# RWKV attention and a gated expert layer: one gate for the last batch instead of two, a rewritten end, and a different place for the key weights' low parts

## The chip, the cores and the metric

One core of a Trainium2 chip runs the whole kernel. The metric is the device time of one execution in microseconds (us). The kernel before takes 455.28 us, the median of three runs (455.16 to 455.67).

## The reference, cut to what matters

The input x has 8 batches of 512 tokens with 512 features, all float32. One layer of attention and one of experts follow each other, each with a residual sum and a normalisation over the features:

```
key = x*mk + shifted*(1-mk);  value = x*mv + shifted*(1-mv);  rec = x*mr + shifted*(1-mr)
k = key @ Wk;  v = value @ Wv;  r = sigmoid(rec @ Wr)
out = wkv(k, v)            # a scan over the tokens: running maximum, numerator, denominator
x = layernorm(x + (r * out) @ Wo)
logits = x @ router.T ;  gate = softmax(logits), kept for the top 2 of 8 experts
h = x @ down.T             # 8 experts x 16 = 128 columns
x = layernorm(x + (silu(h) * gate) @ up)
```

`shifted` is x moved by one token. Ties between experts go to the lower index.

## The kernel before, in words

**Tiles.** A batch has four chunks of 128 features for the attention and four tiles of 128 tokens for the rest. Tiles are counted through: batch 7, the last, has tiles 28 to 31, batch 6 has 24 to 27, batch 5 has 20 to 23. In the code `t5`, `t6`, `t7` are tiles 20, 24 and 28. There are 32 slots, one for each chunk of each batch: slot s does keys, values and receptances of one chunk (`key`, `value`, `rec` on TensorE), the scans over the tokens (VectorE) and the exponentials (ScalarE). Beside it run the output projection and the experts of earlier batches.

**Matmuls.** Batch 0 multiplies in float32 (`whole`), where one product is two passes (the profile counts x2). From batch 1 on, `split` writes each factor as a high part in the type fp32r and a low part, and makes three single passes of it: high by high, low weights by high, high weights by low. For this WKH and WKL must hold the high and low parts of Wk; ScalarE makes WKH, and two VectorE instructions in the slots 0 and 1 make WKL (L1095, `low_weights(lo)` in the VectorE program, 1,024 columns each). The same for Wv and Wr is done by GpSimd (L1283). The mixes (L970) give key, value and rec of the next batch; in slots 0 and 1 VectorE does two key mixes of batch 1 each.

**Order.** Nothing here is scheduled by a planner: each engine runs its own list, written out by hand, and waits on semaphores. An engine never takes a later instruction first, so a wait holds all that is queued behind it.

**The end.** After slot 31 come, written out tile by tile, the projections of tiles 28 to 31 (`project_high`, `project_low`, `project_rest`), their residual sums (`residual`, L991), means and scales (`moments`, `spread`, ScalarE and VectorE), `normalise` (GpSimd, L1264), transposes (`turn`, L443), their copy (`turned`, ScalarE), the product with router and down weights (`hidden`, L461), its copy (`hidden_copy`), and then the gate:

- `ffn_in` (ScalarE): silu's exponentials and the softmax's exponential,
- `gate_scores` (L1022, L1024) and `gate_top` (L1042 to L1060) on VectorE: maximum, ranks of the experts, the weights of the best two,
- `silu` (L1071, L1075): h times sigmoid, times gate; it releases `agd`,
- `ffn_turn` (TensorE, L480) transposes the result, `ffn_out` (ScalarE) copies it to DQ, and `ffn_up` (L513 for batches 6 and 7, L508 to L510 for batch 5) is the product with the up weights, one per tile,
- `residual2` (L996), the second scale (`spread2`, `square2`, `root2`, `moments2`), `normalise2` (GpSimd, L1269) and the store.

The last batch has two gates, one for tiles 28 and 29 and one for 30 and 31: `STEPS` has an entry for each, and `Part(k)` holds their places. Part 6 is batch 6, parts 7 and 8 are the two halves of batch 7.

```python
STEPS = [(b, 0, NT) for b in range(LAST)] + [(LAST, 0, NT // 2), (LAST, NT // 2, NT)]
```

The expert products of batches 5 and 6 also lie in this end, as work for TensorE between the steps of batch 7.

Of the kernel before, what the change touches and what calls it, by code (L numbers as in the profile page):

```python
# [29 lines left out]
def rwkv_moe_postln(nc, x, xt, vec, wk, wv, wr, wo, dr, up, tri, out):  # L30
    with ExitStack() as ctx:
# [83 lines left out]
        STEPS = [(b, 0, NT) for b in range(LAST)] + [(LAST, 0, NT // 2), (LAST, NT // 2, NT)]  # L115
        spare = EX[:, :, :].rearrange("p a t -> p (a t)")

        def step_of(t):
            b, n = divmod(t, NT)
            return b + (b == LAST and n >= NT // 2)  # L120

        class Part:
            def __init__(self, k):
                self.b, lo, hi = STEPS[k]
# [13 lines left out]
                self.turned_at = ((PK[0], PH)[lo // 2] if tail else PP if k == LAST - 1 else PU)[:, 0:128 * (hi - lo)]  # L138
# [4 lines left out]
        PARTS = [Part(k) for k in range(len(STEPS))]  # L143
# [23 lines left out]
        def up_at(t):  # L167
            if t // NT == LAST:
                return tail_bank(t, PT, PK[0], PK[1], PV)
            if t // NT == LAST - 1:  # L170
                return tail_bank(t, PV, PR, PP, PU)
            return tail_bank(t, PU, PT, PK[0], PU) if t // NT == LAST - 2 else PU[:, :]
# [67 lines left out]
        def _(eng):  # L240
# [40 lines left out]
            eng.wait_ge(q["lwk"], 2)  # L281
# [39 lines left out]
        def _(eng):  # L321
# [9 lines left out]
            def split(dst, weights, high, low, u, which, freed):  # L331
# [4 lines left out]
                if b == 1:  # L336
                    eng.wait_ge(q["hw"], which + 1)
                    eng.wait_ge(q[("lwk", "lwv", "lwr")[which]], j + 1 if which else 2)
# [108 lines left out]
            def hidden(t):  # L447
# [5 lines left out]
                elif b == LAST and n == 1:  # L453
                    eng.wait_ge(q["agc"], LAST)
# [10 lines left out]
            def ffn_turn(k):  # L465
                p = PARTS[k]
                eng.wait_ge(q["agd"], k + 1)
                if k > LAST:
                    eng.wait_ge(q["res"], NT * NB)
                elif k == LAST:  # L470
                    eng.wait_ge(q["res2"], NT * (LAST - 2) + 3)
                elif k == LAST - 1:
                    eng.wait_ge(q["res"], NT * LAST + 1)
# [9 lines left out]
            def ffn_up(t):  # L483
# [9 lines left out]
                if b == LAST and n == 0:  # L493
                    eng.wait_ge(q["res2"], NT * (LAST - 2) + 2)
                elif b == LAST and n == NT - 1:
# [5 lines left out]
                elif b == LAST - 2 and 0 < n < NT - 1:  # L501
                    eng.wait_ge(q["res"], NT * LAST + 1 + n)
# [97 lines left out]
        def _(eng):  # L600
# [300 lines left out]
        def _(eng):  # L901
# [166 lines left out]
            def silu(k):  # L1068
                p = PARTS[k]
                eng.wait_ge(q["sg"], k + 1)  # L1070
                eng.tensor_tensor(p.tiled(p.s1), p.tiled(p.s1), p.hs[:, :, 0:EI], ALU.mult).then_inc(q["sh"], 1)  # L1071
                eng.wait_ge(q["sh"], k + 1)
# [19 lines left out]

            def low_weights(lo):
                eng.wait_ge(q["hw"], 1)
                eng.tensor_tensor(WKL[:, lo:lo + 2, :], X1T[:, lo:lo + 2, :], WKH[:, lo:lo + 2, :].bitcast(F32),  # L1095
                                  ALU.subtract).then_inc(q["lwk"], 1)
# [8 lines left out]
            for s in SLOTS:  # L1105
# [38 lines left out]
                if s < 2:  # L1144
                    mixes(1, 0, 2 * s, 2 * s + 1)
# [6 lines left out]
                if s < 2:  # L1152
                    low_weights(2 * s)
# [239 lines left out]
```

## Time and profile before

| | |
|---|---|
| median of three runs | 455.28 us |
| the profiled execution | 455.12 us |
| its span, first to last instruction | 453.3 us |
| TensorE (PE) busy | 442.3 us, 98% |
| VectorE (DVE) busy | 404.6 us, 89% |
| ScalarE (ACT) busy | 363.7 us, 80% |
| GpSimd (POOL) busy | 313.0 us, 69% |
| TensorE's granted clock, mean | 0.995 |

The profile gives for each instruction its start from the span's start and its duration. Instructions of one engine overlap a little: the next one starts before the end of the one before, so the distance of two starts is what a queue pays for one. "L991" is line 991 of the kernel before. A tile's name stands for all buffers of that name (PK for PK0 and PK1). A row "PE PK<-KH,WKH" is a matmul into PK; a float32 matmul counts as two.

### The profile page before, as it was taken

The numbers are of one execution on the slowest core, as the hardware profiler recorded it, in microseconds if no ns is written. First come the engines' busy times: TensorE is split into PE (matmuls) and PEld (weight loads), VectorE is DVE, ScalarE is ACT, GpSimd is POOL, SyncE is SP. The second block draws the span as 40 slices with busy tenths as digits, with TensorE's granted clock in tenths as the row PEclk, the third lists the DMA queues.
The fourth block names the chain that finished last, engine by engine and source line by source line (L and its number), as shares of the span: only waits on it lengthen the run. The fifth ranks groups of instructions, "written<-read, shape, count | busy, mean of one in ns | idle before, by whom it ended". The sixth has DMA issues, their size and how long they took to land. (4 is left out here: it accounts for less than half of the span.)

```text
span 453.3 us, 6683 instructions
## 1 busy us (share of the span) xinstructions
PE 442.3 (98%) x1984; PEld 340.7 (75%) x1984; DVE 404.6 (89%) x614; ACT 363.7 (80%) x810; POOL 313.0 (69%) x298
## 2 busy tenths in 40 slices
PE   8999999999999999999999999999999999999993
PEld 3444667778888888888888888888888888878771
DVE  6999999898888989999899989999899996875985
ACT  7877668877888779888788789888789887668695
POOL 0455786688657997579867898579966794753335
PEclk9999999999999999999999999999999999999998
DMA  8603320042000042003320042100520023400016
GB/s 250 217 1 119 116 69 1 1 140 72 0 1 0 25 163 88 6 0 99 113 71 0 1 158 78 45 0 25 163 94 0 4 68 94 140 1 0 1 48 231
DMA packets 20244, 30.64 MB, mean 68 GB/s; under 512 B 2032, under 2 KB 7152, under 8 KB 20208
## 3 DMA queue, kind: packets, MB, share of 16 engines
q1 hardware_dynamic: 20064, 29.95, 20.5%
q8 instruction: 16, 0.26, 0.2%
q10 hardware_dynamic: 144, 0.26, 0.2%
q14 instruction: 20, 0.16, 0.1%
HBM read 21.82 MB, written 8.39 MB: 67 GB/s over the span
## 5 line engine op out<-in xcount | busy, mean ns | idle before, releaser
L604 ACT ACTIVATE PR<-PR 128x512 f32<-128x512 f32 x128 | 74.5, 582 | 29.0 <-DVE PR L948 9.6
L1255 POOL TENSOR_TENSOR DQ<-DEN,EX 128x512 f32<-128x512 f32 x32 | 41.9, 1310 | 23.6 <-DVE DEN L919 23.6
L1261 POOL TENSOR_SCALAR NM<-SUM,RS 128x1 f32<-128x1 f32 x30 | 7.9, 264 | 59.8 <-ACT RS L604 59.8
L342 PE MATMUL PK<-KH,WKH 128*128 128x512 f32 x112 | 46.5, 415 | 0.4 <-DVE NUM L936 0.4
L970 DVE SCALAR_TENSOR_TENSOR KT<-D,VEC,XT 128x512 f32<-128x512 f32 x56 | 46.3, 874 | 0.0
L342 PE MATMUL PV<-VH,WVH 128*128 128x512 f32 x112 | 45.4, 406 | 0.0
L342 PE MATMUL PR<-RH,WRH 128*128 128x512 f32 x112 | 44.3, 395 | 0.2 <-DVE RW L960 0.2
L348 PE MATMUL PK<-KL,WKH 128*128 128x512 f32 x112 | 44.1, 394 | 0.0
L348 PE MATMUL PV<-VL,WVH 128*128 128x512 f32 x112 | 44.1, 394 | 0.0
L348 PE MATMUL PR<-RL,WRH 128*128 128x512 f32 x112 | 44.0, 393 | 0.0
L343 PE MATMUL PK<-KH,WKL 128*128 128x512 f32 x112 | 43.8, 391 | 0.0
L343 PE MATMUL PR<-RH,WRL 128*128 128x512 f32 x112 | 43.7, 390 | 0.0
L343 PE MATMUL PV<-VH,WVL 128*128 128x512 f32 x112 | 43.7, 390 | 0.0
L1223 POOL TENSOR_TENSOR VL<-KT,VH 128x512 fp32r<-128x512 f32 x28 | 38.9, 1410 | 4.0 <-ACT VH L604 4.0
L1223 POOL TENSOR_TENSOR RL<-D,RH 128x512 fp32r<-128x512 f32 x27 | 39.5, 1492 | 3.0 <-ACT RH L604 2.9
L919 DVE TENSOR_TENSOR_SCAN DEN<-PK,EX 128x512 f32<-128x512 f32 x32 | 38.9, 1217 | 2.6 <-issue 1.4
L604 ACT ACTIVATE EX<-EX 128x512 f32<-128x512 f32 (+1 forms) x66 | 40.3, 610 | 0.0
L936 DVE TENSOR_TENSOR_SCAN NUM<-PK,EX 128x512 f32<-128x512 f32 x32 | 39.2, 1224 | 1.1
L906 DVE TENSOR_TENSOR_SCAN M<-CST,PK 128x512 f32<-128x512 f32 x32 | 38.7, 1211 | 0.0
L604 ACT ACTIVATE PK<-PK 128x512 f32<-128x512 f32 x64 | 38.3, 598 | 0.0
L371 PE MATMUL PP<-WOH,TH 128*128 128x512 f32 x88 | 35.9, 407 | 0.0
L1223 POOL TENSOR_TENSOR KL<-KT,KH 128x512 fp32r<-128x512 f32 x28 | 35.2, 1293 | 0.0
(289 smaller groups left out, 1276.0 us busy)
## 6 DMA issues: line engine op xcount, KB each, us to landing
XT<-in_xt SPq DMA_DIRECT2D x32, 256.0 KB, 3.7
XN<-in_x SPq DMA_DIRECT2D x28, 256.0 KB, 2.7
out<-XN SPq DMA_DIRECT2D x28, 256.0 KB, 2.0
X1T<-in_wo SPq DMA_DIRECT2D x1, 1024.0 KB, 5.5
XT<-in_x SPq DMA_DIRECT2D x4, 256.0 KB, 3.6
out<-XT SPq DMA_DIRECT2D x3, 256.0 KB, 2.3
X1T<-in_wk SPq DMA_DIRECT2D x2, 256.0 KB, 5.0
XN<-in_wv SPq DMA_DIRECT2D x2, 256.0 KB, 5.5
```

Source lines behind the costliest of these rows:

```text
L342: eng.matmul(dst[:, :], wh[:, c, o], high[:, c, :], start=(c == 0), stop=False)
L343: eng.matmul(dst[:, :], wl[:, c, o], high[:, c, :], start=False, stop=False)
L348: last = eng.matmul(dst[:, :], wh[:, c, o], low[:, c, :], start=False, stop=(c == C - 1))
L371: eng.matmul(projected_at(t), high(c), WOH[:, c, :], start=(c == 0), stop=False)
L604: eng.activation(*a, **k).then_inc(q[s], 1)
L906: eng.tensor_tensor_scan(M[:, 1:T + 1], TD[:, j:j + 1].to_broadcast([128, T]), PK[u % 2][:, :], NEG, ALU.add, ALU.max).then_inc(q["m"], 1)
L919: eng.tensor_tensor_scan(DEN[:, 1:T + 1], PK[u % 2][:, :], EX[:, 0, :], 0.0, ALU.mult, ALU.add)\
L936: eng.tensor_tensor_scan(NUM[:, 1:T + 1], PK[u % 2][:, :], EX[:, 0, :], 0.0, ALU.mult, ALU.add)\
L970: eng.scalar_tensor_tensor(out=full(b, which, c), in0=D[:, c, :], scalar=VEC[:, 2 + which, c:c + 1], in1=XT[:, c, 0:T], op0=ALU.mult, op1= ...
L1223: eng.tensor_tensor(lo[:, c, :], full(b, which, c), hi[:, c, :].bitcast(F32), ALU.subtract)\
L1255: eng.tensor_tensor(DQ[:, :], DEN[:, 0:T], EX[:, 1, :], ALU.add).then_inc(q["e"], 1)
L1261: eng.tensor_scalar(NM1[:, col(t)], total, RS1[:, col(t)], scale, ALU.mult, ALU.mult)\
```

## The change

Four things are done, and no arithmetic is left out.

1. **Gate.** `STEPS` goes; batch 7 has one part for its four tiles. `ffn_in`, `gate_scores`, `gate_top`, `silu`, `ffn_turn` and `ffn_out` of batch 7 run once, on operands of twice the columns.
2. **Key weights.** The two VectorE instructions for WKL go. GpSimd makes WKL in slot 0, in four instructions of the form it has for WVL, after the first `denominator` and the differences of batch 1. It first waits until the fourth key mix of batch 1 is done.
3. **Key mixes.** All four key mixes of batch 1 stand in slot 0, none in slot 1. TensorE's keys and the load of Wo wait for four counts of `lwk` instead of two.
4. **End.** The lists of TensorE, ScalarE, VectorE and GpSimd after slot 31 stand in another order, `silu` is cut into `silu_of` and `silu_gated`, and three products use other banks (tile 21 of `ffn_up` PH instead of PT, the transposes of batch 6 PT instead of PP).

The diff, cut to its core:

```diff
-        STEPS = [(b, 0, NT) for b in range(LAST)] + [(LAST, 0, NT // 2), (LAST, NT // 2, NT)]
         def step_of(t):
-            b, n = divmod(t, NT)
-            return b + (b == LAST and n >= NT // 2)
+            return t // NT
...
-                self.turned_at = ((PK[0], PH)[lo // 2] if tail else PP if k == LAST - 1 else PU)[:, 0:128 * (hi - lo)]
+                self.turned_at = (PK[0] if tail else PT if k == LAST - 1 else PU)[:, 0:128 * (hi - lo)]
...
@@ TensorE, end @@
-            ffn_up(t5)
             project_high(t7 + 3)
             project_low(t7 + 3)
             project_rest(t7 + 3)
+            ffn_up(t5)
             turn(t7)
-            ffn_turn(LAST - 1)
+            ffn_up(t5 + 1)
             turn(t7 + 1)
             hidden(t7)
-            ffn_up(t5 + 1)
             turn(t7 + 2)
             hidden(t7 + 1)
+            turn(t7 + 3)
             ffn_up(t5 + 2)
-            turn(t7 + 3)
             hidden(t7 + 2)
+            ffn_turn(LAST - 1)
+            hidden(t7 + 3)
             ffn_up(t5 + 3)
-            hidden(t7 + 3)
-            ffn_up(t6)
+            for t in range(t6, t7):
+                ffn_up(t)
             ffn_turn(LAST)
-            ffn_up(t6 + 1)
-            ffn_up(t6 + 2)
-            ffn_turn(LAST + 1)
-            ffn_up(t6 + 3)
             for t in range(t7, NT * NB):
                 ffn_up(t)
...
@@ ScalarE, end @@
+            spread(t7 + 2)
             turned(t7)
-            spread(t7 + 2)
-            ffn_out(LAST - 1)
-            spread2(t5)
+            spread(t7 + 3)
             turned(t7 + 1)
             hidden_copy(t7)
-            spread(t7 + 3)
             turned(t7 + 2)
             hidden_copy(t7 + 1)
+            turned(t7 + 3)
+            square2(t5, JUNK[:, :])
+            hidden_copy(t7 + 2)
+            ffn_out(LAST - 1)
+            root2(t5, 1)
+            hidden_copy(t7 + 3)
             ffn_in(LAST)
-            turned(t7 + 3)
-            hidden_copy(t7 + 2)
             spread2(t5 + 1)
             square2(t5 + 2, JUNK[:, :])
-            hidden_copy(t7 + 3)
-            ffn_in(LAST + 1)
-            ffn_out(LAST)
             square2(t5 + 3, KT[:, 0, :])
             root2(t5 + 2, 2)
-            ffn_out(LAST + 1)
             spread2(t6, 2)
+            ffn_out(LAST)
             spread2(t6 + 2, 2)
...
@@ VectorE, slots 0 and 1 @@
-                if s < 2:
-                    mixes(1, 0, 2 * s, 2 * s + 1)
+                if s == 0:
+                    mixes(1, 0, 0, 1, 2, 3)
...
-                if s < 2:
-                    low_weights(2 * s)
...
@@ VectorE, end @@
             residual(t7)
-            silu(LAST - 1)
             residual(t7 + 1)
             moments(t7 + 1)
             residual(t7 + 2)
-            residual2(t5)
+            silu_of(LAST - 1)
             residual(t7 + 3)
             moments(t7 + 3)
+            silu_gated(LAST - 1)
+            residual2(t5)
             residual2(t5 + 1)
             moments2(t5 + 1)
+            residual2(t5 + 2)
             gate_scores(LAST)
-            residual2(t5 + 2)
+            residual2(t5 + 3)
             gate_top(LAST)
-            silu(LAST)
-            residual2(t5 + 3)
-            gate_scores(LAST + 1)
-            gate_top(LAST + 1)
-            silu(LAST + 1)
-            for n in range(NT):
-                residual2(t6 + n)
+            residual2(t6)
+            residual2(t6 + 1)
+            silu_of(LAST)
+            silu_gated(LAST)
+            residual2(t6 + 2)
+            residual2(t6 + 3)
...
@@ GpSimd, slot 0 and end @@
+                if s == 0:
+                    eng.wait_ge(q["kt"], 3 * C + C)
+                    low_weights(0, *range(C))
...
-            for n in range(NT - 1):
+            for n in range(NT):
                 normalise(t7 + n)
-            normalise2(t5)
-            normalise(t7 + 3)
-            for t in range(t5 + 1, NT * NB):
+            for t in range(t5, NT * NB):
```

**Where instructions move, VectorE in slots 0 and 1.** Before:

```order
L948 SCALAR_TENSOR_TENSOR PR<-PR,DQ 128x512
L970 SCALAR_TENSOR_TENSOR KT<-D,VEC,XT 128x512 x2
L1095 TENSOR_TENSOR WKL<-X1T,WKH 128x1024
L960 TENSOR_TENSOR RW<-NU,PR 128x512
L919 SCALAR_TENSOR_TENSOR DEN<-PK,EX 128x512
```

Now (the lines have other numbers, the instructions are the same):

```order
L938 SCALAR_TENSOR_TENSOR PR<-PR,DQ 128x512
L960 SCALAR_TENSOR_TENSOR KT<-D,VEC,XT 128x512 x4
L950 TENSOR_TENSOR RW<-NU,PR 128x512
L909 SCALAR_TENSOR_TENSOR DEN<-PK,EX 128x512
```

In slot 0 one WKL instruction is replaced by two mixes; slot 1, which read like the first block too, now has neither.

**VectorE at the end**, from the residual sum of tile 22 (XN1<-PK0) to the last gate's product DEN. EX holds scores and weights of batch 7, NUM the comparisons, M and DEN the two products of silu. Before, the second gate and what is ahead of it:

```order
L1071 TENSOR_TENSOR M<-M,EX 128x256
L1075 TENSOR_TENSOR DEN<-M,EX 128x256
L996 TENSOR_TENSOR XN1<-PU,XN1 128x512
L1022 TENSOR_REDUCE EX<-EX 128x2
L1024 TENSOR_TENSOR EX<-EX 128x16
L1042 TENSOR_TENSOR NUM<-EX 128x128
...
L1060 SCALAR_TENSOR_TENSOR EX<-EX 128x16
L1071 TENSOR_TENSOR M<-M,EX 128x256
L1075 TENSOR_TENSOR DEN<-M,EX 128x256
L996 TENSOR_TENSOR XN0<-PV,XN0 128x512
```

Now:

```order
L986 TENSOR_TENSOR XN1<-PK0,XN1 128x512
L1012 TENSOR_REDUCE EX<-EX 128x4
L1014 TENSOR_TENSOR EX<-EX 128x32
L986 TENSOR_TENSOR XN1<-PU,XN1 128x512
L1032 TENSOR_TENSOR NUM<-EX 128x256
...
L1050 SCALAR_TENSOR_TENSOR EX<-EX 128x32
L986 TENSOR_TENSOR XN0<-PV,XN0 128x512
L986 TENSOR_TENSOR XN0<-PR,XN0 128x512
L1061 TENSOR_TENSOR M<-M,EX 128x512
L1068 TENSOR_TENSOR DEN<-M,EX 128x512
```

Three residual sums (tile 23, then tiles 24 and 25) now stand between the last scores and the product that releases the last transposes.

**TensorE at the end**, its last instructions. Before:

```order
L461 MATMUL PP<-DR,D 128x136 x4
L513 MATMUL PV<-KT,NU 128x512
L480 MATMUL PK<-IDN,DEN 128x128 x2
L513 MATMUL PR<-KT,NU 128x512
L513 MATMUL PP<-KT,NU 128x512
L480 MATMUL PH<-IDN,DEN 128x128 x2
L513 MATMUL PU<-KT,NU 128x512
L513 MATMUL PT<-KT,DQ 128x512
L513 MATMUL PK<-KT,DQ 128x512 x2
L513 MATMUL PV<-KT,DQ 128x512
```

Now:

```order
L459 MATMUL PP<-DR,D 128x136 x4
L502 MATMUL PU<-UPH,AGH 128x512
L503 MATMUL PU<-UPL,AGH 128x512
L504 MATMUL PU<-UPH,AGL 128x512
L507 MATMUL PV<-KT,NU 128x512
L507 MATMUL PR<-KT,NU 128x512
L507 MATMUL PP<-KT,NU 128x512
L507 MATMUL PU<-KT,NU 128x512
L476 MATMUL PK<-IDN,DEN 128x128 x4
L507 MATMUL PT<-KT,DQ 128x512
L507 MATMUL PK<-KT,DQ 128x512 x2
L507 MATMUL PV<-KT,DQ 128x512
```

The product of tile 27 (PU<-KT,NU) stood between the last transposes and the four products of batch 7; now nothing does.

## Rows read from the trace of the kernel before

**Rows 1.** Waits of TensorE over the whole span (us in total, times, longest)

```profile
PE PV L443 <- POOL XT L1264: 0.9, 1, 0.9
PE PK L342 <- DVE NUM L936: 0.4, 1, 0.4
```

**Rows 2.** VectorE in time, start of the program (start us, us, engine, line, operation)

```profile
22.76 1.40 DVE L970 SCALAR_TENSOR_TENSOR KT<-D,VEC,XT 128x512 f32<-128x512 f32 x2
24.08 1.22 DVE L1095 TENSOR_TENSOR WKL<-X1T,WKH 128x1024 fp32r<-128x1024 f32 x1
...
29.80 0.69 DVE L943 TENSOR_TENSOR NU<-NUM,PV 128x512 f32<-128x512 f32 x1
...
36.32 1.23 DVE L919 TENSOR_TENSOR_SCAN DEN<-PK,EX 128x512 f32<-128x512 f32 x1
```

**Rows 3.** TensorE in time, start of the program

```profile
30.95 3.60 PE L328 MATMUL PV<-RW,XN 128*128 128x512 f32 x8
```

**Rows 4.** GpSimd in time, start of the program

```profile
28.38 5.02 POOL L1283 TENSOR_TENSOR WVL<-XN,WVH 128x512 fp32r<-128x512 f32 x4
```

**Rows 5.** ScalarE in time, start of the program

```profile
35.65 0.59 ACT L604 ACTIVATE PK<-PK 128x512 f32<-128x512 f32 x1
```

**Rows 6.** TensorE in time, end of the program

```profile
428.65 0.60 PE L443 MATMUL PK<-IDN,XT 128*128 128x128 f32 x4
...
430.56 0.63 PE L443 MATMUL PV<-IDN,XT 128*128 128x128 f32 x4 [0.88 <-POOL XT L1264]
...
438.23 1.02 PE L513 MATMUL PV<-KT,NU 128*128 128x512 f32 x2
...
442.69 1.02 PE L513 MATMUL PT<-KT,DQ 128*128 128x512 f32 x2
443.54 1.88 PE L513 MATMUL PK<-KT,DQ 128*128 128x512 f32 x4
445.26 1.02 PE L513 MATMUL PV<-KT,DQ 128*128 128x512 f32 x2
```

**Rows 7.** VectorE in time, end of the program

```profile
421.78 0.41 DVE L1042 TENSOR_TENSOR KT<-HS 128x256 f32<-128x256 f32 x1
422.11 1.54 DVE L1043 TENSOR_TENSOR KT<-HS 128x256 f32<-128x256 f32 x1
...
425.14 0.68 DVE L991 SCALAR_TENSOR_TENSOR XT<-PP,XT 128x512 f32<-128x512 f32 x1
...
425.75 0.68 DVE L1071 TENSOR_TENSOR KT<-KT,HS 128x512 f32<-128x512 f32 x1
426.47 0.69 DVE L1075 TENSOR_TENSOR KT<-KT,GS 128x512 f32<-128x512 f32 x1
...
435.75 0.28 DVE L1042 TENSOR_TENSOR NUM<-EX 128x128 f32<-128x128 f32 x1
...
437.29 0.42 DVE L1071 TENSOR_TENSOR M<-M,EX 128x256 f32<-128x256 f32 x1
...
441.07 0.42 DVE L1075 TENSOR_TENSOR DEN<-M,EX 128x256 f32<-128x256 f32 x1
...
445.46 0.69 DVE L996 TENSOR_TENSOR XT<-PK,XT 128x512 f32<-128x512 f32 x1 [0.17 <-PE PK L513]
```

**Rows 8.** ScalarE in time, end of the program

```profile
430.96 0.58 ACT L604 ACTIVATE NU<-PP 128x512 f32<-128x512 f32 x1
...
438.43 0.28 ACT L604 ACTIVATE EX<-PP 128x136 f32<-128x136 f32 x1 [0.23 <-PE PP L461]
```

**Rows 9.** The chain that ended last, its last row

```profile
449.12 0.72 ACT XT L604
```

**Rows 10.** GpSimd in time, end of the program

```profile
437.68 1.04 POOL L1269 TENSOR_SCALAR XN<-XN,RS,ZERO 128x512 f32<-128x512 f32 x1 [2.85 <-ACT RS L678]
```

**Rows 11.** After the last matmul: stretch, busy PE, PEld, DVE, ACT, POOL, granted clock, DMA

```profile
448.00:449.00 1.00, 0.00 (x0) 0.00 (x0) 0.96 (x3) 0.49 (x3) 1.00 (x2) 1.00 0.95 352
449.00:450.00 1.00, 0.00 (x0) 0.00 (x0) 0.00 (x0) 0.81 (x2) 0.63 (x1) 0.54 0.64 240
```

More of the change, by code:

```diff
@@ L112, in col @@
             return slice(i, i + 1)
-        STEPS = [(b, 0, NT) for b in range(LAST)] + [(LAST, 0, NT // 2), (LAST, NT // 2, NT)]
         spare = EX[:, :, :].rearrange("p a t -> p (a t)")
         def step_of(t):
-            b, n = divmod(t, NT)
-            return b + (b == LAST and n >= NT // 2)
+            return t // NT
         class Part:
             def __init__(self, k):
-                self.b, lo, hi = STEPS[k]
+                self.b, lo, hi = k, 0, NT
                 self.tiles, self.n = range(NT * self.b + lo, NT * self.b + hi), hi - lo
@@ L137, in __init__ @@
                 self.agt = (DQ if tail else NU if k == LAST - 1 else AGH)[:, 128 * lo:128 * hi]
-                self.turned_at = ((PK[0], PH)[lo // 2] if tail else PP if k == LAST - 1 else PU)[:, 0:128 * (hi - lo)]
+                self.turned_at = (PK[0] if tail else PT if k == LAST - 1 else PU)[:, 0:128 * (hi - lo)]
             def tiled(self, a):
                 return a.rearrange("p (n h) -> p n h", n=self.n)
-        PARTS = [Part(k) for k in range(len(STEPS))]
+        PARTS = [Part(k) for k in range(NB)]
         def tail_bank(t, *banks):
@@ L171, in up_at @@
                 return tail_bank(t, PV, PR, PP, PU)
-            return tail_bank(t, PU, PT, PK[0], PU) if t // NT == LAST - 2 else PU[:, :]
+            return tail_bank(t, PU, PH, PK[0], PU) if t // NT == LAST - 2 else PU[:, :]
         MEASURED = [NT * (LAST - 2) + 1, NT * LAST + 2, NT * LAST + 3]
@@ L280, in _ @@
             eng.dma_start(TRI[:, :], tri).then_inc(q["tri"], 16)
-            eng.wait_ge(q["lwk"], 2)
+            eng.wait_ge(q["lwk"], C)
             eng.wait_ge(q["k"], C)
@@ L337, in split @@
                     eng.wait_ge(q["hw"], which + 1)
-                    eng.wait_ge(q[("lwk", "lwv", "lwr")[which]], j + 1 if which else 2)
+                    eng.wait_ge(q[("lwk", "lwv", "lwr")[which]], j + 1)
                 for c in range(C):
@@ L453, in hidden @@
                 elif b == LAST and n == 1:
-                    eng.wait_ge(q["agc"], LAST)
+                    eng.wait_ge(q["res"], NT * LAST + 1)
                 elif b == LAST:
@@ L467, in ffn_turn @@
                 eng.wait_ge(q["agd"], k + 1)
-                if k > LAST:
-                    eng.wait_ge(q["res"], NT * NB)
-                elif k == LAST:
+                if k == LAST:
                     eng.wait_ge(q["res2"], NT * (LAST - 2) + 3)
                 elif k == LAST - 1:
-                    eng.wait_ge(q["res"], NT * LAST + 1)
+                    eng.wait_ge(q["res"], NT * LAST + 2)
                 elif k == LAST - 2:
@@ L492, in ffn_up @@
                     eng.wait_ge(q["agl"], k + 1)
-                if b == LAST and n == 0:
-                    eng.wait_ge(q["res2"], NT * (LAST - 2) + 2)
-                elif b == LAST and n == NT - 1:
+                if b == LAST and n == NT - 1:
                     eng.wait_ge(q["res2"], NT * (LAST - 1) + 1)
@@ L501, in ffn_up @@
                 elif b == LAST - 2 and 0 < n < NT - 1:
-                    eng.wait_ge(q["res"], NT * LAST + 1 + n)
+                    eng.wait_ge(q["res"], NT * LAST + 5 - n)
                 elif LAST - 2 <= b < LAST and n:
@@ L1066, in gated_low, with silu_of @@
                    .then_inc(q["agl"], 1)
-            def silu(k):
+            def silu_of(k):
                 p = PARTS[k]
@@ L1071, in silu, with silu_gated @@
                 eng.tensor_tensor(p.tiled(p.s1), p.tiled(p.s1), p.hs[:, :, 0:EI], ALU.mult).then_inc(q["sh"], 1)
+            def silu_gated(k):
+                p = PARTS[k]
                 eng.wait_ge(q["sh"], k + 1)
@@ L1091, in _ @@
             eng.tensor_scalar(QB, CC, -1.0, CLIP, ALU.mult, ALU.add).then_inc(q["cc"], 1)
[L1093 to L1096, printed above, removed]
             first_mixes(0, 0, 1)
@@ L1278, in low_weights @@
             def low_weights(i, *blocks):
-                stage, high, low, done = ((XN[0], WVH, WVL, "lwv"), (XN[1], WRH, WRL, "lwr"))[i - 1]
+                stage, high, low, done = ((X1T, WKH, WKL, "lwk"), (XN[0], WVH, WVL, "lwv"), (XN[1], WRH, WRL, "lwr"))[i]
                 eng.wait_ge(q["hw"], i + 1)
```

## The prediction

> **What bounds the kernel now.** I read TensorE's waits first: in the whole span it waits hardly at all, and the two longest waits inside it are 0.9 and 0.4 us [rows 1]. So up to about 428 us the kernel is TensorE's stream, and its matmuls don't change. A change of VectorE's list can only gain there what those waits hold. Then the chain that ended last, which closes with ScalarE's scaling of tile 31 at 449.12 [rows 9]; followed back it runs over VectorE's residual sums and TensorE's last four products, the first at 442.69 [rows 6]. VectorE's sum of tile 30 at 445.46 waited for them [rows 7]. So the end is set by when those products start, and the second gate's DEN, done at 441.07 + 0.42 = 441.49 [rows 7], is what lets them.
>
> **The start.** Removed from VectorE: two WKL instructions of 1.22 us. Moved from slot 1 to slot 0: two mixes, 1.40 us a pair [rows 2]. Slot 0 pays 1.4 - 1.2 = 0.2 us more, slot 1 about 2.6 us less. Neither reaches the end:
> - The 0.2 us: VectorE's NU of slot 1 ends at 29.80 + 0.69 = 30.49 [rows 2], and the values that wait for it start at 30.95 [rows 3]. With 0.2 us more it is still 0.25 us early. If that cover is gone, TensorE waits by the excess, at most 0.2 us in each of a few slots; I take 0, with +0.3 as the upper end.
> - The 2.6 us: VectorE's next scan is DEN at 36.32, and ScalarE's exponential that it needs ends at 35.65 + 0.59 = 36.24 [rows 2, 5]. VectorE becomes free at 34 and waits. I take 0; the lower end is the 0.4 us wait for VectorE later on [rows 1].
> - GpSimd: four WKL instructions of the form of the WVL ones, 5.02 us for four [rows 4]. They start when the fourth mix ends, 22.76 + 4 x 0.7 = 25.5, and end at 30.5; the DQ instruction behind them, then WVL, end near 31.8 and 36.8, 3.4 us later than now (28.38 + 5.02 = 33.4). The keys that need WKL come only after four slots of batch 0, and the next work of GpSimd hangs on DEN at 36.32 + 1.23. The load of Wo waits for `lwk` and for the keys of slot 3, and the latter stays last. The cover here is over 0.5 us at each place. Cost 0.
>
> **The end, TensorE up to the last hidden product.** From tile 28's transposes at 428.65 to the first product of batch 6 at 438.23 TensorE does, in another order, the same instructions as after the change [rows 6]; ahead of 428.65 too, since only `ffn_up(t5)` and the projection of tile 31 change places. Of these 9.58 us, 0.88 is a wait for GpSimd's normalised tile 29 [rows 6]. It falls away: ScalarE no longer copies tile 28's transposes and squares tile 30 ahead of what GpSimd needs, and a 0.8 us product fills the gap (it waits some 0.2 us for the residual sum of tile 31). By the distances of the starts I also count 0.5 us of small waits for copies less, since each copy now lies ahead of two instructions. The block takes 8.2 us, and hidden(31) is now followed by one 0.8 us product. So its copy, which ended at 438.43 + 0.28 = 438.71 [rows 8], ends at **436.6**, 2.1 us earlier; 437.1 if the small waits stay.
>
> **The end, VectorE to the last gate's product.** In front of DEN, from the copy on:
> - scores 0.4 us, to 437.0;
> - residual2 of tile 23, 0.6 us (a sum of this size costs the queue 425.75 - 425.14 = 0.61 [rows 7]), to 437.6;
> - gate_top on four tiles: batch 6's took from 421.78 to 425.14 = 3.36 us, with one comparison at 1.54 where its twin took 0.41 [rows 7]. That one ran beside a GpSimd instruction on two tensors, which the new place does not have: 3.36 - 1.13 = 2.23 us, to 439.85;
> - residual2 of tiles 24 and 25, 1.2 us, to 441.05;
> - the two silu products on 512 columns, 426.47 - 425.75 + 0.69 = 1.41 us [rows 7], to **442.46**.
>
> ScalarE's part (`ffn_in`) needs 2.5 us from 436.6 and is done at 439.2, beside gate_top. So `agd` comes 442.46 - 441.49 = 0.97 us later than the second gate's does now. Two gates cost VectorE more in all than one, but the last of two needs only 441.49 - 438.71 = 2.8 us behind the last copy, and this one 5.9.
>
> **From there to the end.** Four transposes, 0.60 us, then the copy of 512 columns, 0.58 [rows 6, 8], with 0.1 us between: the first product of batch 7 starts at 443.8 in place of 442.69, **+1.1 us**. TensorE's four products of batch 6 run straight behind the block, 436.9 + 4 x 0.86 = 440.3, so it is idle from then on; now the product of tile 27 covers the second gate's copy, and that makes the 0.1 us on top. The four products, 0.85 us each (443.54 - 442.69 [rows 6]), the sums, moments, root, scaling and the store follow unchanged, so 1.1 us reaches the end. GpSimd's last stores come no later than they do now.
>
> **Sum.** 0 + 1.1 us on the profiled 455.12 gives 456.2; the median of the runs is 0.16 above that execution, so for medians **456.4 us**, 0.25% slower. The line between this and no change is 0.2%, 0.9 us, about what a measurement of this kernel can tell. The term's own bounds: the copy at 437.1 adds 0.5; without the wait at 437 for the sum of tile 23 it is 0.6 less. This case alone spans 455.8 to 457.3.
>
> **Rivals.**
> - *The gate is cheaper than its columns.* The two-tile gate_top took 437.29 - 435.75 = 1.54 us [rows 7]. If four tiles cost the same, 0.7 us are saved; with silu nearer its small form (0.78 for two), 1.3. The sum is then -0.2: no change, 455.1. Against it: the same instructions took 0.41 on 256 columns and 0.28 on 128 [rows 7]. Chance 0.18.
> - *The head start carries through, faster.* The place is VectorE between the last copy and DEN. If besides the cheap gate the sums of tiles 24 and 25 cost nothing, since VectorE would have waited there for ScalarE's sigmoid anyway, `agd` comes at 439.9, and the end 1.4 us sooner: 453.9. It decides from `agd` earlier than 441.4. For it: the last copy is 2.1 us earlier. Against it: by the durations ScalarE is done before gate_top. Chance 0.10.
> - *TensorE's clock.* The new gap, 440.3 to 443.8 with only transposes in it, is longer than any before the last product now. In the trace the granted clock is still 1.00 in 448 to 449, more than 1.7 us after the last matmul (445.26 + 1.02 = 446.28 [rows 6]), and 0.54 in 449 to 450 [rows 11]. If it falls in the gap, the four products take 1.7 us each in place of 0.86: +3.4 more, 459.8. Against it: the gap is broken by transposes. Chance 0.12.
> - *The port of VectorE and GpSimd.* GpSimd's `normalise2` of tile 22 becomes ready at 441.4, between the two silu products. In the trace that same meeting, GpSimd at 437.68 between M at 437.29 and DEN, stretched GpSimd to 1.04 us and left VectorE's products alone (M 0.42, as in the other gate's DEN) [rows 7, 10]. So I take 0. But VectorE did lose 1.13 us once to a GpSimd instruction [rows 7], so this might be +0.7, 457.1; chance 0.05.
>
> The Trainium skill (SBUF — State Buffer, section "SBUF: two separate sides") has a VectorE instruction with two SBUF inputs and a GpSimd instruction exclude each other for the whole of one, the first to start going first. By that rule the second product could wait for all of a 0.8 us `normalise2`; the 1.54 us comparison agrees with the rule, and the row at 437.68 shows GpSimd as the one that waits. By the same rule WKL on GpSimd would cost VectorE something only beside mixes, and none is left there.
>
> **How the numbers follow.** The main case has 0.55, of which 0.08 stays within 0.9 us. Slower: 0.47 + 0.12 + 0.05 = 0.64. Within 0.2%: 0.08 + 0.18 = 0.26. Faster: 0.10. The range 454.8 to 457.7 takes in the main case, the cheap gate and the port, and leaves out the clock and most of the faster case, 0.2 in all.
>
> **What would show it.** Right: TensorE without the 0.9 us wait at 430; the last copy near 436.6; VectorE waiting before the scores; gate_top some 2.2 us; DEN ending near 442.5; a TensorE gap of about 2 us before the last four transposes; the first of the last four products at 443.8; unchanged starts of the slots of batch 1. Wrong: DEN before 441.5, matmuls of batch 7 at twice their duration, or TensorE waiting for NU or WKL before 60 us.

## The result, and the profile after

The changed kernel takes **459.33 us** (median of 6 runs, 458.33 to 460.17) beside 455.29 us for the kernel before on the same chip (6 runs, 454.99 to 455.67): ratio 1.0085, 95% interval 1.0067 to 1.0102. So it is slower, by nearly four times what was predicted (4.0 us, not 1.1), and outside the range. The profiled execution took 460.08 us, its span is 458.3; the kernel before has 455.12 and 453.3.

The 5.0 us between the two spans, read from the start of tile 28's transposes on, since up to there TensorE does the same matmuls:

| stretch | before | after | difference | predicted |
|---|---|---|---|---|
| span's start to tile 28's transposes | 428.65 | 429.02 | +0.37 | 0 |
| from there to the first product of batch 7 | 14.04 | 16.33 | +2.29 | +1.1 |
| from there to ScalarE's last scaling | 6.43 | 9.18 | +2.75 | 0 |
| from there to the span's end | 4.18 | 3.77 | -0.41 | 0 |

The -0.41 fits the stores: from the last scaling on fewer are left. Before, the shares of the DMA engines in the four microseconds from 449 on add up to 3.0 (0.64, 1.02, 1.03, 0.35), now in the four from 454 on to 2.1 (0.00, 0.74, 1.02, 0.33).

TensorE's waits in the changed kernel (us in total, times, longest), against [rows 1]:

```profile
PE PK L476 <- DVE DEN L1068: 2.7, 1, 2.7
...
PE PT L507 <- ACT DQ L595: 0.7, 1, 0.7
PE PK L340 <- DVE NUM L926: 0.4, 1, 0.4
PE PH L502 <- DVE XT L981: 0.4, 1, 0.4
```

The wait of 0.9 us for GpSimd's normalised tile 29 is gone, as predicted. A wait of 2.7 us for the gate's product and one of 0.7 for its copy have taken its place. TensorE in time, to be read against [rows 6] (a bracket at the end of a row is the engine's idle time just ahead of it, and what ended it):

```profile
429.02 0.60 PE L441 MATMUL PK<-IDN,XT 128*128 128x128 f32 x4
430.04 0.47 PE L502 MATMUL PH<-UPH,AGH 128*128 128x512 f32 x1 [0.42 <-DVE XT L981]
...
437.67 1.02 PE L507 MATMUL PV<-KT,NU 128*128 128x512 f32 x2
...
440.25 1.02 PE L507 MATMUL PU<-KT,NU 128*128 128x512 f32 x2
443.94 0.72 PE L476 MATMUL PK<-IDN,DEN 128*128 128x128 f32 x4 [2.68 <-DVE DEN L1068]
445.35 2.07 PE L507 MATMUL PT<-KT,DQ 128*128 128x512 f32 x2 [0.69 <-ACT DQ L595]
447.21 3.62 PE L507 MATMUL PK<-KT,DQ 128*128 128x512 f32 x4
450.62 1.33 PE L507 MATMUL PV<-KT,DQ 128*128 128x512 f32 x2
```

TensorE stands still from 440.25 + 1.02 = 441.27 to 443.94. The first product of batch 7 starts at 445.35 in place of 442.69, and then two products of two matmuls take 2.07 and 1.33 us and four matmuls 3.62, where [rows 6] have 1.02, 1.02 and 1.88. VectorE, against [rows 7]:

```profile
428.27 1.02 DVE L1061 TENSOR_TENSOR KT<-KT,HS 128x512 f32<-128x512 f32 x1
429.21 0.68 DVE L981 SCALAR_TENSOR_TENSOR XT<-PH,XT 128x512 f32<-128x512 f32 x1
```
```profile
437.49 0.19 DVE L1012 TENSOR_REDUCE EX<-EX 128x4 f32<-128x32 f32 x1 [1.92 <-ACT EX L595]
...
438.60 0.41 DVE L1032 TENSOR_TENSOR NUM<-EX 128x256 f32<-128x256 f32 x1
...
440.83 0.68 DVE L986 TENSOR_TENSOR XN<-PV,XN 128x512 f32<-128x512 f32 x1
...
442.03 0.68 DVE L1061 TENSOR_TENSOR M<-M,EX 128x512 f32<-128x512 f32 x1
442.75 1.14 DVE L1068 TENSOR_TENSOR DEN<-M,EX 128x512 f32<-128x512 f32 x1
...
447.46 0.69 DVE L986 TENSOR_TENSOR XT<-PT,XT 128x512 f32<-128x512 f32 x1 [2.37 <-PE PT L507]
```

After it waited for the last hidden copy (ScalarE's, below), VectorE doesn't pause until DEN ends, at 442.75 + 1.14 = 443.89. Later it waits 2.37 us for the slow products. ScalarE's last copy and its last scaling, against [rows 8, 9], and GpSimd's scaling of tile 21 (its first row) and of tiles 22 and 23 (the second):

```profile
437.17 0.28 ACT L595 ACTIVATE EX<-PP 128x136 f32<-128x136 f32 x1
...
454.53 0.72 ACT L595 ACTIVATE XT<-XT,RS 128x512 f32<-128x512 f32 x1
```
```profile
440.61 0.79 POOL L1256 TENSOR_SCALAR XN<-XN,RS,ZERO 128x512 f32<-128x512 f32 x1 [2.58 <-ACT RS L669]
442.42 2.11 POOL L1256 TENSOR_SCALAR XN<-XN,RS,ZERO 128x512 f32<-128x512 f32 x2 [1.03 <-ACT RS L680]
```

The stretches of the end (busy PE, PEld, DVE, ACT, POOL, then TensorE's granted clock, DMA share, GB/s), against [rows 11]:

```profile
443.00:444.00 1.00, 0.06 (x1) 0.06 (x2) 1.00 (x2) 0.82 (x4) 1.00 (x2) 1.00 0.04 12
444.00:445.00 1.00, 0.66 (x4) 0.36 (x4) 1.00 (x2) 0.44 (x2) 1.00 (x2) 0.70 0.70 262
445.00:450.00 5.00, 4.65 (x6) 2.07 (x7) 1.47 (x3) 2.75 (x10) 2.55 (x4) 0.50 0.65 240
450.00:451.00 1.00, 1.00 (x2) 0.45 (x2) 0.13 (x1) 0.82 (x3) 0.00 (x0) 0.50 0.30 111
451.00:452.00 1.00, 0.95 (x2) 0.00 (x0) 0.97 (x2) 0.20 (x1) 0.70 (x1) 0.88 0.00 0
```

The granted clock is 1.00 (2.4 GHz) until 444, falls within the next microsecond to 0.50 (1.2 GHz), and stays there until past 451: six of the eight last matmuls run wholly at half the clock. That is the rival that had 0.12.

### The profile page after: what moved, and what is told of

The parts are those of the page before. It is cut to its first block, busy times and chain, and to the rows that moved or that the text cites. A ratio compares the mean times of both kernels' runs of the same rounds, so it can differ in the third digit from the quotient of the medians.

```text
span 458.3 us, 6662 instructions
## 1 busy us (share of the span) xinstructions
PE 445.9 (97%) x1984; PEld 342.5 (75%) x1984; DVE 401.5 (88%) x599; ACT 363.8 (79%) x804; POOL 318.8 (70%) x302
## 4 chain that ended last, share of the span: by engine, by line
PE 79%; DVE 4%; ACT 1%; issue 1%; POOL 1%; ACTq 0%
PE PH L459 6%; PE PV L346 5%; PE PV L340 5%; PE PV L341 5%; PE PK L340 5%; PE PK L346 5%; PE PR L346 5%; PE PK L341 5%; PE PR L341 5%; PE PR L340 5%; PE PP L369 4%; PE PP L374 4%; PE PP L370 4%; PE PT L441 3%; PE PP L389 2%
```

## The experiments

Two questions were open. Is the clock the cause of the 2.75 us, and nothing else? And what is the remaining 2.29 us made of, of which 1.1 was predicted? All the times below are medians; the kernel before took 455.2 to 455.4 in each group. "Behind tile 28" is the distance from the start of tile 28's transposes, which takes out what the start of the program adds or saves.

**The changed kernel again**, beside the next three on one chip.

> The changed kernel once more, to see whether its runs fall into two groups. Theory (the granted clock falls in the gap ahead of the last four products): runs of two kinds, near 458.4 and near 460.1 us, the slower kind with a mean clock of 0.989 and with the four products at some 1.8 us each. Rival (the time comes from the order of work and the shared port alone): one group, and a run with a high mean clock is as long as the others. If a profile of the faster kind is caught, the first of the four products starts where it does in the slow one, near 445.3, and the products are faster.

460.09 us (460.09 to 460.12), ratio 1.0104 (1.0091 to 1.0117), mean granted clock 0.988 in every run. All four runs were of the longer kind. The 458.3 to 458.6 of three of the first runs didn't come up; those had a mean clock of 0.992 to 0.995.

**Unread products in the gap.**

```diff
             for t in range(t6, t7):
                 ffn_up(t)
+            for _ in range(3):
+                eng.matmul(PH[:, :], IDN[:, :], UPT, start=True, stop=True)
             ffn_turn(LAST)
```

> Three float32 products whose result nobody reads (into bank PH, 0.86 us each) run on TensorE between its last product of batch 6 and the four last transposes, where it waited 2.7 us. Clock theory: the clock stays at 1.00, the four products take 0.86 us each, so 3.4 us come back from a run of the slow kind and the time is 456.5 to 457 us in one group. Rival (order and port cost the whole): nothing comes back, 459.3. A third view (filling delays the transposes): first product later than 445.3.

457.14 us (456.88 to 457.21), ratio 1.0038 (1.0026 to 1.0049). TensorE:

```profile
440.94 2.74 PE L586 MATMUL PH<-KT,IDN 128*128 128x512 f32 x6
443.77 0.66 PE L476 MATMUL PK<-IDN,DEN 128*128 128x128 f32 x4
445.12 1.13 PE L507 MATMUL PT<-KT,DQ 128*128 128x512 f32 x2 [0.69 <-ACT DQ L597]
```

The granted clock stays at 1.00 there, the transposes take 0.66 and the first product 1.13. It starts 16.27 us behind tile 28, as in the changed kernel (16.33): work that nobody reads, put where TensorE was idle, moves no other step, and takes 2.95 us off. From the first product to ScalarE's last scaling it is 451.66 - 445.12 = 6.54 us, against 6.43 before and 9.18 in the changed kernel: the clock explains the slower products. What is left, 1.9 us against the kernel before, comes with the later release of the last transposes; the next runs take that apart.

**The start change alone**, on the kernel before (all key mixes of slot 0 together, the key lows on GpSimd; the end as before).

> The kernel before with the change of the start alone (all four key mixes in slot 0, WKL on GpSimd behind them). My theory: no change, 455.3 us, -0.1 to +0.3. Rival (the start is what costs part of the 4 us, as TensorE's values start 0.6 us later in the profile of the changed kernel): 455.9 or more. If the 0.6 us in that profile is only the first eight matmuls (6.27 in place of 5.20 us, whose work did not change), the start varies from run to run in the kernel before as well.

454.98 us (454.72 to 455.79), ratio 0.9993 (0.9984 to 1.0002): no change that this measurement can tell. The order of the end is that of [rows 6], and so are the distances: 443.36 - 429.32 = 14.04.

```profile
429.32 0.60 PE L443 MATMUL PK<-IDN,XT 128*128 128x128 f32 x4
...
443.36 1.02 PE L513 MATMUL PT<-KT,DQ 128*128 128x512 f32 x2
```

**The silu products ahead of two residual sums** (the changed kernel, no filler).

```diff
+            silu_of(LAST)
+            silu_gated(LAST)
             residual2(t6)
             residual2(t6 + 1)
-            silu_of(LAST)
-            silu_gated(LAST)
```

(ScalarE's `ffn_out(LAST)` goes ahead of `spread2(t6, 2)` likewise.)

> The changed kernel with the two silu products of batch 7 ahead of the residual sums of tiles 24 and 25 on VectorE, and the copy of the last transposes ahead of the squares of those tiles on ScalarE. Order theory: the last product of the gate ends 1.2 us earlier and misses the GpSimd instructions that stretched it to 1.14 us, so 1.2 + 0.45 us are gained by the order alone. Clock theory: the wait ahead of the last transposes shrinks from 2.7 to about 1.0 us and the clock does not fall, so another 3.4 us: 455.5 to 456.2 us in all. If the clock falls in spite of it: 457.5 to 458.5.

457.27 us (456.11 to 457.69), ratio 1.0037 (1.0025 to 1.005). The profiled run is the shortest, 456.11:

```profile
442.10 0.66 PE L476 MATMUL PK<-IDN,DEN 128*128 128x128 f32 x4 [1.45 <-DVE DEN L1068]
443.44 1.12 PE L507 MATMUL PT<-KT,DQ 128*128 128x512 f32 x2 [0.69 <-ACT DQ L595]
```
```profile
440.21 1.10 DVE L1061 TENSOR_TENSOR M<-M,EX 128x512 f32<-128x512 f32 x1
441.35 0.69 DVE L1068 TENSOR_TENSOR DEN<-M,EX 128x512 f32<-128x512 f32 x1
```

The two sums cost about what the prediction had for them (1.2): the first product comes 443.44 - 428.41 = 15.03 us behind tile 28, 1.30 sooner. The gap is 1.45 us in place of 2.68, and in this run the clock stayed at 1.00 through it. It didn't in all: of the six runs two took 456.1 and 456.3, and four 457.0 to 457.7. That the clock fell in those four is read from their times alone: no trace of one was kept, and their mean clock of 0.994 hardly differs from the 0.995 of the profiled run. DEN is back at 0.69, and now the product before it, M, has the 1.10: GpSimd's scaling of tile 21 meets that one.

**GpSimd held back** (on the filled kernel: GpSimd waits for the last gate's product before tile 22).

```diff
                 if t not in FINISHED:
+                    if t == t5 + 2:
+                        eng.wait_ge(q["agd"], NB)
                     normalise2(t)
```

> The changed kernel with the three unread products in TensorE's gap (the clock held, 457.14), and GpSimd made to wait for the last gate's product (agd at NB) before normalise2 of tile 22. Theory: in the changed kernel DEN takes 1.14 us in place of 0.69 because GpSimd's normalise2 runs at the same time; with GpSimd held back DEN is 0.69 again, the last four transposes start 0.45 us sooner, and the time is 456.7, ratio 1.0031. Rival: DEN is long for another reason (ScalarE's reads, TensorE's fillers), stays at 1.14, and the time stays at 457.1.

456.70 us (456.28 to 457.32), ratio 1.0034 (1.0022 to 1.0046).

```profile
441.98 0.69 DVE L1070 TENSOR_TENSOR DEN<-M,EX 128x512 f32<-128x512 f32 x1
```

DEN takes 0.69: the stretch was GpSimd's. The first product comes 444.19 - 428.24 = 15.95 us behind tile 28, 0.32 sooner than in the filled kernel, not 0.45: DEN is done at 442.67, but the three unread products keep TensorE until the transposes start at 442.91.

**`silu_of` of batch 6 behind tile 31's residual sum** (on the filled kernel).

```diff
-            silu_of(LAST - 1)
             residual(t7 + 3)
             moments(t7 + 3)
+            silu_of(LAST - 1)
```

> The same base (changed, three unread products), but silu_of of batch 6 behind the residual sum and moments of tile 31 in VectorE's list. Theory: the last hidden copy is late by up to 0.48 us because VectorE does that product, 1.02 us beside a GpSimd instruction, ahead of tile 31's residual sum, and TensorE's ffn_up waits 0.42 for that sum; moved behind, the wait goes, the copy and all behind it come about 0.4 us sooner: 456.7. Rival: the wait only changes its cause (the later copy, or silu_gated and ffn_out of batch 6, now late for its own products), and the time stays at 457.1.

456.62 us (456.34 to 457.06), ratio 1.0031 (1.002 to 1.0042).

```profile
428.33 0.60 PE L441 MATMUL PK<-IDN,XT 128*128 128x128 f32 x4
428.76 0.47 PE L502 MATMUL PH<-UPH,AGH 128*128 128x512 f32 x1
```

`ffn_up` follows the transposes after 0.43 us, without the wait (in the changed kernel 1.02, with 0.42 of wait); the last copy starts 436.12 - 428.33 = 7.79 us behind tile 28 in place of 8.15, the first product 15.91 in place of 16.27.

**All of these at once**, with `ffn_up` of tile 27 behind the last transposes, where it covers their copy, and two unread products. GpSimd waits for the last gate's product already before tile 21 here, and ScalarE's copy goes ahead of `spread2(t6, 2)` again. TensorE's list:

```diff
-            for t in range(t6, t7):
+            for t in range(t6, t6 + 3):
                 ffn_up(t)
+            eng.wait_ge(q["res2"], NT * (LAST - 2) + 3)
+            for _ in range(2):
+                eng.matmul(PH[:, :], IDN[:, :], UPT, start=True, stop=True)
             ffn_turn(LAST)
+            ffn_up(t6 + 3)
```

> All mends at once on the changed kernel: both silu products of the last gate ahead of the residual sums of tiles 24 and 25; silu_of of batch 6 late; GpSimd waits for the last gate's product before normalise2 of tile 21; two unread products in the gap instead of three; and ffn_up of tile 27 behind the last gate's transposes, where it covers ScalarE's copy of them. The theory's terms, each from a run so far: clock 2.95, the two sums 1.2 to 1.4, late copy 0.45, stretched product 0.45. From 457.14 with the clock held: minus 1.2, 0.4, 0.45 gives 455.1, no change against before (ratio 0.9997). Rival: the terms do not add, since the residual sums moved behind the gate now come late for the products of batch 7 that reuse their banks: then 456 or more.

455.43 us (455.14 to 456.06), ratio 1.0007 (0.9999 to 1.0016): as the kernel before.

```profile
441.43 0.66 PE L476 MATMUL PK<-IDN,DEN 128*128 128x128 f32 x4 [0.17 <-DVE DEN L1072]
...
442.78 1.11 PE L507 MATMUL PT<-KT,DQ 128*128 128x512 f32 x2
```

The terms add at the first product: it is 442.78 - 428.52 = 14.26 us behind tile 28, against 14.04 before and 16.27 with the filler alone, so 2.0 us sooner, and 1.2, 0.36 and 0.45 were expected. Of the 2.0 the time shows 1.7 (457.14 to 455.43).

**Two gates in the new order**: the end as changed, but the last batch's gate split again into pairs, `silu_of` of batch 6 late, and ScalarE's squares of tiles 20 and 21 behind the gates. No unread products. `STEPS`, the banks of the last batch's transposes and TensorE's two `ffn_turn` are as in the kernel before. VectorE's list:

```diff
+            gate_scores(LAST)
+            gate_top(LAST)
             residual2(t5 + 2)
-            gate_scores(LAST)
+            silu_of(LAST)
+            silu_gated(LAST)
+            gate_scores(LAST + 1)
             residual2(t5 + 3)
-            gate_top(LAST)
-            residual2(t6)
-            residual2(t6 + 1)
-            silu_of(LAST)
-            silu_gated(LAST)
+            gate_top(LAST + 1)
+            silu_of(LAST + 1)
+            silu_gated(LAST + 1)
+            residual2(t6)
+            residual2(t6 + 1)
```

> The changed kernel's new order of the end up to the last hidden product, but the one gate split again into two of two tiles, as before, and ScalarE's squares of tiles 20 and 21 behind the last gate. Theory: what the one gate costs is that all four tiles' work waits for the last copy; with two gates the first is done ahead of it, and the first of the last four products starts 12.7 to 14 us behind tile 28's transposes in place of 14.04 before and 16.3 now: 454.0 to 455.2, ratio 0.997 to 1.000. Rival: ScalarE (four exponentials, two copies and the postponed squares) becomes the bound at the end, and the time is 456 or more.

455.54 us (455.29 to 456.02), ratio 1.0006 (0.9997 to 1.0015). TensorE, VectorE and ScalarE:

```profile
440.18 0.44 PE L480 MATMUL PH<-IDN,DEN 128*128 128x128 f32 x2 [0.37 <-DVE DEN L1076]
...
441.32 1.02 PE L511 MATMUL PT<-KT,DQ 128*128 128x512 f32 x2
```
```profile
448.66 0.79 DVE L1005 TENSOR_SCALAR XT<-XT,RS 128x512 f32<-128x512 f32 x1 [1.41 <-ACT RS L676]
```
```profile
448.98 0.72 ACT L602 ACTIVATE XT<-XT,RS 128x512 f32<-128x512 f32 x1
```

The first product is 441.32 - 428.58 = **12.74** us behind tile 28: 1.30 sooner than before, 3.59 sooner than in the changed kernel (16.33), and 1.52 sooner than with one gate and every mend (14.26). So the new order, with two gates, gains 1.30 us at this place; joining the gate loses 1.52 of the 3.59, and the other 2.07 are what the mends of the run before took back. But the gain of 1.3 us stops at ScalarE: VectorE stands 1.41 us waiting for its root, and the last scaling starts 20.40 behind tile 28, against 20.47 before. The time lies between the theory's and the rival's; the mechanism at the end is the rival's.

**The same, with the end balanced anew.**

```diff
-        MEASURED = [NT * (LAST - 2) + 1, NT * LAST + 2, NT * LAST + 3]
+        MEASURED = [NT * (LAST - 2) + 1, NT * LAST + 1, NT * LAST + 2, NT * LAST + 3]
...
-            spread2(t7, 2)
-            spread2(t7 + 2)
-            spread2(t7 + 3)
+            spread2(t7)
+            spread2(t7 + 1, 3)
```

(VectorE takes `moments2(t7 + 1)` behind `residual2(t7 + 1)`.)

> Two gates in the new order, as in the run before, with the end balanced anew: tile 29's second moments move from ScalarE (square and sum) to VectorE, which waited 1.41 us there for ScalarE's root, and ScalarE takes the roots of tiles 29 to 31 in one pair of instructions in place of three. Theory: in that run the last products end 1.5 us sooner than before, and ScalarE, busy without a gap from 440.65 to 448.98, hands none of it on; relieved of a square (0.7 us) and of two pairs (0.5 us each), its last scaling starts 0.5 to 0.7 us sooner: 454.9, ratio 0.9987, and no more than the stores allow. Rival: the stores, four in the last 3 us, are the bound, and the time stays at 455.5.

455.29 us (454.93 to 455.88), ratio 0.9998 (0.9989 to 1.0007). The last scaling starts 448.93 - 428.98 = 19.95 us behind tile 28, 0.45 sooner than in the run before, but the span's end comes 453.8 - 448.93 = 4.87 us behind it, where the kernel before has 4.18. The DMA engines (last two columns, share and GB/s) in the last stretches:

```profile
450.00:451.00 1.00, 0.00 (x0) 0.00 (x0) 0.00 (x0) 0.00 (x0) 0.17 (x1) 0.50 0.94 344
451.00:452.00 1.00, 0.00 (x0) 0.00 (x0) 0.00 (x0) 0.00 (x0) 0.00 (x0) 0.50 1.01 383
452.00:453.00 1.00, 0.00 (x0) 0.00 (x0) 0.00 (x0) 0.00 (x0) 0.00 (x0) 0.50 0.92 346
```

They are nearly full until 453, while in the kernel before, where tile 28 came 0.33 us earlier, their share in 452 to 453 is 0.35. GpSimd ends its last scaling 21.2 us behind tile 28 (before: 21.0), so the store behind that one comes no sooner, however early ScalarE is. The rival, the stores as the bound, fits; that a better spread of the stores would bring the rest was not tried.

**One unread product in place of three.**

> The changed kernel with one unread product in TensorE's gap in place of three, so that about 2 us stay idle ahead of the last transposes and 0.7 behind them. Theory: the clock falls with the length of the idle stretch, not because of the products' place; with 1.45 + 0.69 us idle (the silu products first) some runs lost about 1.4 us and some nothing, so here a part of the 2.95 us stays: 458 to 459, in two kinds of runs. Rival: any real product inside the gap keeps the clock: 457.1 in every run.

457.26 us (457.04 to 458.75), ratio 1.005 (1.0036 to 1.0065). Four runs took 457.0 to 457.3, two 458.5 and 458.8; the profiled one is of the latter:

```profile
443.60 0.66 PE L476 MATMUL PK<-IDN,DEN 128*128 128x128 f32 x4 [1.81 <-DVE DEN L1070]
444.94 1.97 PE L507 MATMUL PT<-KT,DQ 128*128 128x512 f32 x2 [0.69 <-ACT DQ L597]
```
```profile
444.00:445.00 1.00, 0.31 (x4) 0.07 (x2) 0.74 (x2) 0.71 (x2) 1.00 (x3) 1.00 0.58 217
445.00:446.00 1.00, 1.00 (x2) 0.48 (x3) 0.00 (x0) 1.00 (x4) 0.70 (x1) 0.54 0.90 330
```

With 1.81 + 0.69 us idle the clock fell to 0.54 in 445 to 446, a microsecond later than in the changed kernel, and came back earlier. A real product in the gap doesn't hold the clock by being there: what stays idle behind it still counts. The rival, 457.1 in every run, fell. Of the theory the two kinds of runs held, but not the 458 to 459: four of six runs lost nothing that shows. The changed kernel without any filler kept three of its five runs on the same chip (below), so these six don't show that one unread product makes a fall rarer.

**The changed kernel on this chip too.**

> The changed kernel itself on this chip, beside the other two. The runs so far gave 460.1 or 458.4 us and nothing between. Theory: the two kinds differ in TensorE's clock alone, and a profile of the shorter kind shows the last products partly at the full rate. 460.1 in most runs; a 458.4 run may or may not come up.

457.02 us (456.83 to 460.19), ratio 1.006 (1.0035 to 1.0084). Neither the theory's 460.1 nor its 458.4: three runs took 456.8 to 457.0 at a mean clock of 0.997 or 0.998, two 459.6 and 460.2 at 0.991 and 0.988. The first three have the time and the mean clock of the filled kernel; none of them was profiled. So by the times the same program with the same gap lost 3 us in two runs and nothing in three; the profile shown is of a run that lost:

```profile
443.52 1.12 PE L476 MATMUL PK<-IDN,DEN 128*128 128x128 f32 x4 [2.69 <-DVE DEN L1068]
```
```profile
443.00:444.00 1.00, 0.48 (x2) 0.48 (x3) 1.00 (x3) 0.53 (x4) 1.00 (x1) 0.50 0.22 84
```

Here the clock was already down when the last transposes ran: 1.12 us, against 0.66 in the filled kernel. The granted clock is 0.50 in all of 443 to 444, and the last product of batch 6 had ended at 439.81 + 1.02 = 440.83: it fell within 2.2 us of it, sooner than in the profile of [rows 11], where it fell some 2.7 us behind the last matmul.

## Why the prediction was wrong

It had the direction and the place. The number failed, since the largest term, the clock, was put down as a rival and left out of the range; of the terms up to the first product four were short as well.

- **The start, at 0: right.** Alone it gives a ratio of 0.9993 (0.9984 to 1.0002). Neither the GpSimd work nor the longer slot 0 shows. The 0.37 us by which tile 28 comes later in the profiled run is within what profiles of the changed start differ by: the twelve of them have tile 28's transposes between 428.24 and 429.32, with the 428.65 of the kernel before inside. TensorE's first eight matmuls, whose work didn't change, took 5.20 us before, 6.27 after, and 4.74 and 6.21 in two other runs of the changed start.
- **The wait of 0.9 us, gone: right.** The 0.2 us expected in its place are 0.42 (`PE PH L502`). The step that failed is the cover: the prediction didn't count that `silu_of` of batch 6 stands ahead of tile 31's residual sum on VectorE and takes 1.02 us beside GpSimd. That and small waits that stayed make the last hidden copy end 8.43 us behind tile 28, not 7.95: **+0.48**, of which moving that product took back 0.36.
- **From the copy to DEN: 1.15 and 2.23 us where 1.0 and 2.23 were predicted.** The four-tile `gate_top` is exact: it runs from 438.60 to 440.83. The 1.54 us comparison that the prediction took out of batch 6's figure did run beside GpSimd:

```profile
422.07 1.30 POOL L1248 TENSOR_TENSOR KL<-RW,KH 128x512 fp32r<-128x512 f32 x1 [2.24 <-ACT KH L604]
```

  With the 2.23 the cheap-gate rival falls. The two residual sums took 1.20, and moving them away gained 1.30. So the second rival, the head start, in which they hide, falls too.
- **The silu products at 1.41: wrong by 0.45.** DEN takes 1.14, and 0.69 with GpSimd held back. "So I take 0" was the failed step: the meeting of [rows 10] was read as harmless because there GpSimd had lost. GpSimd had come second there; here it is ahead of DEN. Its scaling of tile 22, the first of the two in the row at 442.42, began beside the silu product M (442.03) and took 0.93 us, asked for alone, where the one at 440.61 took 0.79; it ended at 443.35. DEN had begun at 442.75 and ended at 443.89, 0.54 us behind GpSimd's end, where it takes 0.69 alone: it had waited for nearly all of the scaling. The Trainium skill (SBUF — State Buffer, section "SBUF: two separate sides") states this for a VectorE instruction with two inputs in SBUF: the one that starts first has the port for its whole instruction. These rows agree with it in who waits, in both orders; by the starts and durations of the rows DEN would have ended at 443.35 + 0.69 = 444.04, 0.15 us later than it did. In the same rows VectorE's sums that read a product from PSUM (440.83, 0.68) aren't stretched beside GpSimd's 440.61.
- **Behind DEN, 1.34 predicted, 1.46 measured.** In all 1.1 + 0.48 + 0.15 + 0.45 + 0.12 = 2.3, and 2.29 is what the table has. With the clock held the kernel takes 456.8 to 457.2 us: inside the range, some 0.6 above the forecast. That it comes so close is in part luck: the first product is 2.2 us late and not 1.1, and the stores give back 0.44 at the end (from the last scaling to the span's end 455.4 - 451.66 = 3.74 us with the filler, 4.18 before), which the prediction had at 0.
- **The clock: 0.12 for what happened, in whole or in part, in 12 of the changed kernel's 15 runs.** The rival was priced at +3.4 and cost 2.95; its 459.8 stands beside 459.33. What failed is how [rows 11] were read. They show 1.00 for 448 to 449 and 0.54 for 449 to 450, that is, a fall some 2.7 us or more behind the last matmul, which had ended at 446.28. The failed step is the overlap: the prediction took only the first half of it ("still 1.00 after 1.7 us") as speaking against, while its own gap, 440.3 to 443.8, was 3.5 us long. And the transposes that were to break the gap stand near its end: even ahead of them it had 440.3 to 442.5. So the rows gave no ground for a chance of 0.12. The Trainium skill (TensorE: Matmul & The Clock Gate, section "Part 1: The HAM clock gate") has the half rate as what an idle TensorE goes to and the two levels as the only ones; the granted clock of 0.50 and matmuls of twice the duration agree.

Why one gate comes later than the last of two: its work is cheap in sum, but all of it waits for the last tile's hidden product. With two, half the gate is done by then, and the first gate's copy and product fill TensorE while the second is worked out. The first product of batch 7 comes 16.33 us behind tile 28 in the changed kernel, 14.26 with one gate and the mended order, and 12.74 with two gates in the new order. Of these 3.59 us the joined gate itself has 1.52 (the two runs behind this also differ in the unread products and in where ScalarE has two squares). The other 2.07 are the order around it: the two residual sums ahead of the silu products (1.2 to 1.3), GpSimd's scaling beside DEN (0.3 to 0.45) and `silu_of` of batch 6 (0.36). Where the clock falls, 2.95 come on top. The kernel before, with its older order, has 1.30 of the 3.59 too. In the whole time the 1.52 us don't show: one gate in the mended order, with two unread products, takes 455.43 us, two gates take 455.54 and the kernel before 455.39; with two gates ScalarE's queue holds the end, and behind it, as far as the runs go, the stores. So what made the changed kernel slow is the gap that it left TensorE and the order around the gate; that joining the gate by itself costs time was not shown.

## What to carry to other kernels

Before work near the end is joined or moved, write down how long TensorE will stand idle just before its last products, and compare that with how long the clock outlived the last matmul in the traces at hand. If the gap comes near it, put the products behind it at twice their duration in one end of the range. A single trace is no safe measure: here it showed 2.7 us, another run had lost the clock within 2.2, and by their times even runs with 1.45 + 0.69 us idle lost some of it. Cheap remedies, in the order in which I would try them: shorten the gap by putting first, on the engine that TensorE waits for, what TensorE needs; move real products into it; and only then unread ones. Of two engines that share a port, ask which will start first, not which lost last time. A gain on TensorE is worth only what the next engine's queue lets through.

## What was not expected of the hardware

- The same program with the same idle gap of 2.7 us kept the clock in three runs (456.8 to 457.0) and lost it in others (459.6 to 460.2), with 458.3 to 458.6 between. A gap of 1.45 + 0.69 us cost part of it in four runs of six, one of 1.81 + 0.69 in two of six; with 0.17 us idle none of eleven runs showed it. These counts go by the times of the runs; traces were kept of three runs of the changed kernel, all with the loss, and of one run of each of the others. The chip may have a part: the changed kernel lost the clock in four of four runs on the chip of the first experiments and in two of five on that of the last three. What decides it within one program these runs don't settle.
- Six half-rate matmuls passed before the full rate came back, although TensorE was busy throughout once they had begun: 0.50 from 445.0 to 451.0, 1.00 from 452. The first repeat of the changed kernel shows the same; in the last repeat the full rate is back in 449 to 450, and with one unread product in 448 to 449.
- The eight matmuls at the program's start take between 4.74 and 6.27 us from run to run. Little of that reaches the end: tile 28's transposes start at 428.85 in the run with 4.74, and at 429.02 in the one with 6.27.
